# A graph-network kernel on one core: the three bf16 parts of the summed edge features are added once, and each graph-layer tile takes one edge product instead of two

## The reference, cut to what matters

```python
def _L2_gnn_ref(node_features, edge_index, edge_features, Ws, bs, gammas, betas):
    src, tgt = (edge_index[0], edge_index[1])
    x = node_features
    for i in range(NUM_LAYERS):                      # 3 layers
        msg = jnp.concatenate([x[src], edge_features], axis=-1)   # 10000 x (512 + 64)
        msg = msg @ Ws[i] + bs[i]
        agg = jax.ops.segment_sum(msg, tgt, num_segments=n)
        x = x + agg
        x = jax.nn.relu(_layer_norm(x, gammas[i], betas[i]))
    return x
```

## Time and profile before

| What | Value |
|---|---|
| Device time, median of 3 runs | 2346.91 us (2346.05 to 2350.74) |
| The profiled execution's own time | 2350.67 us |
| Its span in the trace | 2348.8 us |
| Mean granted clock of TensorE | 0.949 of full speed |
| TensorE (PE) busy | 2180.5 us, 93% |
| VectorE (DVE) busy | 1042.6 us, 44% |
| ScalarE (ACT) busy | 730.8 us, 31% |
| GpSimd (POOL) busy | 558.1 us, 24% |

### The profile page before, as it was taken

One profiled execution on the slowest core, in us unless ns is written; L12 is line 12 of the kernel. 1 busy time (PEld: TensorE's weight loads), 2 busy tenths in 40 slices (PEclk: granted clock), 3 DMA queues, 4 the chain that ended last, 5 costly groups with the idle time before them and its releaser, 6 DMA issues.

```text
span 2348.8 us, 21972 instructions
## 1 busy us (share of the span) xinstructions
PE 2180.5 (93%) x8167; PEld 1257.5 (54%) x8167; DVE 1042.6 (44%) x2142; ACT 730.8 (31%) x1221; POOL 558.1 (24%) x469
## 2 busy tenths in 40 slices
PE   6899886788899999997899999999999999999998
PEld 3576663677444555443455555555555544444443
DVE  8896675787323332344445345345344410000002
ACT  1576554676421210002143233233243111111110
POOL 4677764333211100010202202202202110022202
PEclk9999997787899969998899999999999899999999
DMA  9522204431020110005101101101101477787732
GB/s 344 159 34 34 28 4 108 129 86 57 1 94 19 54 54 20 1 0 187 64 10 55 67 10 59 64 9 59 54 1 54 172 262 302 284 303 307 288 152 70
DMA packets 61668, 238.26 MB, mean 101 GB/s; under 512 B 23375, under 2 KB 28451, under 8 KB 39436
## 3 DMA queue, kind: packets, MB, share of 16 engines
q1 hardware_dynamic: 32058, 169.04, 20.1%
q0 software_dynamic: 26336, 62.19, 8.6%
q10 hardware_dynamic: 3168, 5.63, 0.7%
HBM read 204.84 MB, written 31.96 MB: 101 GB/s over the span
## 4 chain that ended last, share of the span: by engine, by line
PE 64%; DVE 11%; issue 10%; POOL 4%; PEld 4%; DMA 3%; ACT 3%; SPq 0%; ACTq 0%; PEldq 0%; DVEq 0%; POOLq 0%
PE PS L995 10%; PE PS L725 10%; PE PS L718 7%; PE PS L1387 7%; PE PS L1396 6%; PE PS L1425 6%; PE PS L1293 3%; POOL pair_scores L1969 2%; PE PS L1033 2%; PE PS L1273 2%; DMA pair_scores<-TS,SIDX 2%; PE PS L736 1%; PEld PS L718 1%; DVE AR L2394 1%; PE PS L869 1%
## 5 line engine op out<-in xcount | busy, mean ns | idle before, releaser
L1940 POOL TENSOR_TENSOR RSTD<-VE,HALF 125x1 f32<-125x1 f32 x100 | 81.8, 818 | 1033.7 <-DVE VE L2101 1033.7
L995 PE MATMUL PS<-XT,WR 128*128 128x500 f32 (+2 forms) x992 | 235.5, 395 | 8.4 <-ACT XT L1493 4.4
L869 PE MATMUL PS<-HR,HOT 125*125 125x512 f32 x800 | 214.2, 416 | 19.2 <-DVE HOT L2245 17.6
L725 PE MATMUL PS<-WR,XT 128*125 128x512 f32 (+1 forms) x464 | 206.5, 592 | 14.1 <-DVE AR L2684 7.3
L2899 DVE TENSOR_TENSOR AR<-AR,PS 128x512 f32<-128x512 f32 (+1 forms) x44 | 30.3, 688 | 404.9 <-PE PS L1396 404.9
L995 PEld LDWEIGHTS PS<-XT,WR 128*128 128x128 f32 x992 | 145.7, 194 | 89.1 <-issue 74.5
L869 PEld LDWEIGHTS PS<-HR,HOT 125*125 125x125 f32 x800 | 148.6, 194 | 62.1 <-DVE HOT L2245 20.3
L1958 POOL DMA_INDIRECT pair_sums<-CW,SIDX x80 | 137.4, 1718 | 56.4 <-DMA pair_sums<-CW,SIDX 24.0
L725 PEld LDWEIGHTS PS<-WR,XT 128*125 128x125 f32 x464 | 86.8, 194 | 102.4 <-issue 85.5
L718 PE MATMUL PS<-XT,WR 128*128 128x113 f32 (+3 forms) x432 | 125.5, 447 | 1.8 <-DVE CW L2209 1.3
L2123 DVE TENSOR_TENSOR AR<-PS,AR 125x512 f32<-125x512 f32 x55 | 38.0, 692 | 189.3 <-PE PS L725 106.5
(11 more groups left out here) (422 smaller groups left out, 3995.1 us busy)
## 6 DMA issues: line engine op xcount, KB each, us to landing
WR<-in_qkv SPq DMA_DIRECT2D x12, 1024.0 KB
WR<-in_omm SPq DMA_DIRECT2D x12, 1024.0 KB
pair_scores<-CNT SPq DMA_DIRECT2D x1, 12212.0 KB, 36.0
AR<-pair_scores SPq DMA_DIRECT2D x5, 2187.5 KB
AR<-in_x_a SPq DMA_DIRECT2D x10, 1024.0 KB, 9.5
AR<-in_x_b SPq DMA_DIRECT2D x10, 1024.0 KB, 4.9
AR<-in_x_c SPq DMA_DIRECT2D x10, 1024.0 KB, 7.3
WR<-in_x_a SPq DMA_DIRECT2D x8, 1024.0 KB, 8.8
```

The source lines that it names most:

```text
L725: last = mm(s.ap[0:P, 0:cols], lhs, rhs, start=(k == 0), stop=(k == len(pairs) - 1))
L869: last = mm(DIFF[m % 4], HOT[g % 2][0:P, k, tile(j)], HR[0:P, k, :, b, :], start=(k == 0 and b == 0), stop=(k == NT - 1 and b == 1))
L995: last = mm(by_tile(s)[:, t0:t1, :], w[:, k, 128 * m:128 * (m + 1)], XT[:, k, P * t0:P * t1].rearrange("p (c n) -> p c n", n=P), start=(k ...
L1940: g.tensor_tensor(RSTD[:, t:t + 1], VE[:, t:t + 1], HALF[:, :], ALU.pow)\
```

## The change

ScalarE copies only the middle part to `EA1`, which shrinks to 64 rows at partitions 0 to 63, and `EA2` as before. VectorE waits for `graph_taken` and then makes two additions of 64 by 625 elements in place: the middle part to the low part in `EA2`, then the high part, read from PSUM. Each signals the new semaphore `graph_joined`, and TensorE waits for both in place of `graph_taken`. In the layers the product of line 1187 is gone, and the one with `EA2` opens each tile's sum. Two of the three loads of the edge rows are gone. The five semaphores `sums_in` become three, used in turn. The three parts are now added in float32 on VectorE in the place of TensorE's accumulation. The rounding of the first weights stays one unbroken loop.

```diff
--- before.py
+++ after.py
@@ -225,7 +225,7 @@
         G = G_ROWS[0:P, :, :]
 
 
-        EA1 = passing("EA1", [128, N])
+        EA1 = passing("EA1", [DH0, N])
         CONDR = sb("CONDR", [128, N], F32R)
         EA2 = sb("EA2", [128, N])
         with nc.sbuf_tensor("MODW_high", [128, D], F32):
@@ -431,9 +431,9 @@
         onehot_ready, onehot_used = sem("onehot_ready"), sem("onehot_used")
         graph_filled, graph_taken = sem("graph_filled"), sem("graph_taken")
         high_ready, middle_ready, low_ready = sem("high_ready"), sem("middle_ready"), sem("low_ready")
-        last_ready = sem("last_ready")
+        last_ready, graph_joined = sem("last_ready"), sem("graph_joined")
         edge_read = sem("edge_read")
-        sums_in = [sem(f"pair_sums_in_{t}") for t in range(NT)]
+        sums_in = [sem(f"pair_sums_in_{b}") for b in range(3)]
         sums_merged = sem("sums_merged")
         pairs_in = [sem("pair_scores_in_0"), sem("pair_scores_in_1")]
         scaled_ready, raw_filled, raw_taken = sem("scaled_ready"), sem("raw_filled"), sem("raw_taken")
@@ -565,7 +565,7 @@
                     for lo, hi in zip(WIDE_ROWS, WIDE_ROWS[1:]):
                         sp.dma_start(SUMS_IN[t][b][lo:hi].rearrange("p q c -> p (q c)"),
                                      pair_sums[b][N * (P * t + lo):N * (P * t + hi), :].rearrange(
-                                         "(p q) c -> p (q c)", q=N)).then_inc(sums_in[t], 16)
+                                         "(p q) c -> p (q c)", q=N)).then_inc(sums_in[t % 3], 16)
 
             def scores_of(t):
                 for lo, hi in zip(WIDE_ROWS, WIDE_ROWS[1:]):
@@ -601,8 +601,7 @@
                   (WR[:, 0, 2, 0:D], a["W2"])])
             load([mat(1, j, x) for j, x in enumerate(("e_W1", "e_W3", "e_W2"))])
             load([mat(0, j, "Wtop", j) for j in range(3)])
-            load([(WR[0:64, 1, 0, 0:3 * D], a["Wbot"]), (WR[64:128, 1, 0, 0:3 * D], a["Wbot"]),
-                  (WR[0:65, 1, 1, 0:3 * D], a["Wlast"])])
+            load([(WR[0:65, 1, 1, 0:3 * D], a["Wlast"])])
             load([mat(0, 0, "f_W1"), mat(0, 1, "f_W2"), (WR[0:8, 0, 2, 0:D], a["f_b2"])])
             def mod_rows(i, j, landed_in):
                 for r in range(4):
@@ -902,7 +901,7 @@
                                                    HR[0:P, t, h, :, :].rearrange("p b d -> p (b d)").bitcast(F32), ID[0:P, 0:P])
                     last.then_inc(s.filled, 1)
             all_taken("T")
-            pe.wait_ge(graph_taken, 1)
+            pe.wait_ge(graph_joined, 2)
 
 
             def quantized(u):
@@ -1181,11 +1180,10 @@
                     gathered.append((s, n.now(s.filled)))
                 if l == 0:
                     weights(0, 3)
-                    weights(1, 3)
+                    weights(1, 1)
                 for t in range(NT):
                     o = fill("N")
-                    mm(o.ap[0:P, :], EA1[:, tile(t)], WR[:, 1, 0, D * l:D * (l + 1)], start=True, stop=False)
-                    mm(o.ap[0:P, :], EA2[0:65, tile(t)], WR[0:65, 1, 1, D * l:D * (l + 1)], start=False, stop=False)
+                    mm(o.ap[0:P, :], EA2[0:65, tile(t)], WR[0:65, 1, 1, D * l:D * (l + 1)], start=True, stop=False)
                     for f in range(K4):
                         if t == 0:
                             copied(gathered[f])
@@ -1598,7 +1596,7 @@
                     fn(rows[:, :, tile(t)], s.ap[:, 0:4 * P].rearrange("p (h n) -> p h n", h=4), ACT.Copy)\
                         .then_inc(s.taken, 1)
             act.wait_ge(graph_filled, 1)
-            fn(EA1[:, :], PS[:, 2 * BANK:2 * BANK + N], ACT.Copy)
+            fn(EA1[0:DH0, :], PS[DH0:2 * DH0, 2 * BANK:2 * BANK + N], ACT.Copy)
             fn(EA2[0:65, :], PS[0:65, 4 * BANK:4 * BANK + N], ACT.Copy).then_inc(graph_taken, 1)
 
 
@@ -2303,7 +2301,7 @@
             for b in range(PARTS):
                 v.memset(S2[b][:, :, 64:65], 1.0)
             def merge(t):
-                dve.wait_ge(sums_in[t], 64)
+                dve.wait_ge(sums_in[t % 3], 64 * (t // 3 + 1))
                 one, two = SUMS_IN[t]
                 v.tensor_tensor(CNT[:, t, :], one[:, :, 0], two[:, :, 0], ALU.add)
                 v.tensor_tensor(G[:, t, :], one[:, :, 1], two[:, :, 1], ALU.add).then_inc(sums_merged, 1)
@@ -2344,6 +2342,10 @@
                     PRODUCT[rows, :].unsqueeze(2).unsqueeze(3).broadcast_to([DH0, HEADS0, 2, DH0]),
                     ALU.mult).then_inc(uv_ready, 1)
             psum.skip(T=2 * NT)
+            dve.wait_ge(graph_taken, 1)
+            for k, part_ in enumerate((EA1[0:DH0, :], PS[0:DH0, 2 * BANK:2 * BANK + N])):
+                v.tensor_tensor(EA2[0:DH0, :], EA2[0:DH0, :], part_, ALU.add).then_inc(graph_joined, 1)
+                dve.wait_ge(graph_joined, k + 1)
 
             def left(u):
```

## The result

| | before | after |
|---|---|---|
| median of four runs each (us) | 2346.77 | 2334.0 |
| lowest to highest (us) | 2346.05 to 2350.74 | 2332.2 to 2335.7 |
| profiled execution: its time, its span (us) | 2350.67, 2348.8 | 2333.17, 2331.4 |
| busy TensorE / VectorE / GpSimd (us) | | 2167.1 / 1043.0 / 553.4 |
| three graph layers, first edge product to the issue of `in_f_W` (us) | 120.86 | 107.98 |

What follows compares the result with a forecast made beforehand. TensorE was taken to bound the graph layers; -13.0 us for the products and +0.5 us for the additions gave -12.5 us, from a median of 2346.91 to 2334.4 us. The range was 2329 to 2341 us.

Steps and rivals of the forecast that it cites:

- The products: Graph layers, TensorE: 15 products go, each priced 0.87 us from start to start, -13.0 us.
- 65 rows at the price of 128: Graph layers: the product that stays has 65 rows for 128 and takes the same 592 ns, so nothing more is won.
- The copy and VectorE in the first two layers: First two layers: ScalarE's copy stays hidden by 2.5 us, VectorE's wait shrinks from 1.42 to 0.55 us; cost 0.
- The third layer: Third layer: VectorE becomes slower, `Y` comes 2.6 us later against TensorE, 5.7 us of slack remain; cost 0.
- if the wait for the weights shrinks by more than a us: Behind the layers: sign that the forecast is wrong, `Y` or something else having taken over.
- The loads and the semaphores: Two edge-row loads gone, TensorE waiting nowhere for their batch; three semaphores for five reads change no wait; cost 0.
- The additions at the hand-over: Behind the edge loop: 1.7 us of additions covered; GpSimd's stores stretched, +0.5 us, bounds -0.3 and +1.5.
- The cover: Hand-over: first kept group ready before GpSimd takes it at 382.61; 4.6 us of 6.4 left after the additions.
- Contention: Rival at the hand-over: additions and moved rounding block GpSimd's stores in full, +1.5 for +0.5, 2335.4 us; chance 8%.
- VectorE in the third layer: Rival: the tiles of `Y` are waited for behind the layers, 2.6 us given back, 2337.0 us; chance 7%.
- The clock of the heads: Rival, attention heads, 400 to 600 us: grant falls from 0.77 to below 0.71 and eats the gain; chance 3%.
- The product hidden: Rival in the layers: the removed product lay beside something ending at the same time, TensorE waits instead, 2346.9 us; chance 5%.

Runs made afterwards that it cites:

- e3: Kernel before without the 128-row `EA1` product in all three layers, no additions, all loads kept: layers 107.99 us, median 2328.95 us, ratio to before 0.9943.
- e9: Changed kernel with its 65-row `EA2` product issued twice per tile: layers 120.86 us, median 2341.32 us, ratio to before 0.9991.
- e1: Changed kernel with a 64-row `EA1` product put back per tile ahead of the `EA2` one: layers 126.51 us, median 2354.04 us, ratio to before 1.0052.
- e2: Kernel before with the `EA1` product left out in the third layer only, no additions: layers 116.56 us, median 2339.93 us, ratio to before 0.999.
- e8: Kernel before with the two additions, TensorE's wait and the three semaphores, both products and all loads kept: layers 120.86 us, median 2342.64 us, ratio 1.0005.
- e7: Changed kernel with the 65-row edge product in fp32r, sums and weights rounded: layers 98.67 us, median 2323.05 us, ratio to before 0.9916.
- e7b: Changed kernel with the edge product in fp32r, run a second time: layers 98.67 us, median 2320.84 us, ratio to before 0.9905.
- e0: Changed kernel unedited, run again for comparison within its group: layers 107.99 us, median 2326.09 us, ratio to before 0.9938.
- e6: Kernel before with the `EA1` product left out in the first two layers only, no additions: layers 112.27 us, median 2335.51 us, ratio to before 0.9974.
- e4: Changed kernel with six additions in place of two, TensorE waiting for the last: layers 107.98 us, median 2329.58 us, ratio to before 0.9925.
- e5: Changed kernel with 14 additions in place of two, TensorE waiting for the last: layers 107.98 us, median 2338.89 us, ratio to before 0.9988.
- e0b: Changed kernel unedited, a third time, for comparison within its group: layers 107.99 us, median 2328.71 us, ratio to before 0.9937.

## Why the prediction was right, and where it was off

The forecast was 2334.4 us, the measured median 2334.0. That they lie 0.4 us apart is in part luck: the interval of the ratio goes from -17.4 to -6.6 us, and the profiled execution, forecast at 2338.2, took 2333.17. What bears the forecast out is the length of the layers, -12.88 us for -13.0.

- **The products, -13.0 us:** the layers show -12.88, and `e3` -12.87 with nothing else changed; `e9` takes them back with one product of 0.87 us. That the records' sum (17.8 us) is too much and start to start counts is confirmed: 15 x 0.86.
- **65 rows at the price of 128:** holds, by `e9`. With 64 rows ahead of 65 it fails (`e1`).
- **The copy and VectorE in the first two layers, 0:** TensorE is never idle there, and VectorE's wait is 0.56 us, forecast 0.55.
- **The third layer, 0:** VectorE is the slower engine, as forecast. The third tile of `Y` was ready at 1053.51 + 0.54 = 1054.05 and turned at 1059.43, so 5.4 us of slack remained, forecast 5.7. `e2` shows the third layer's part, 4.30 us, arriving alone. The test I named for the opposite was badly put: "if the wait for the weights shrinks by more than a us" came true (6.53 to 4.05) and the theory stood. A wait can shrink because a shorter one has moved in ahead of it; the test should have been the distance from the issue to the first product, 9.22 and then 8.77 us.
- **The loads and the semaphores, 0:** the layers' first tiles are without idle time and `e8` with the semaphores is level with before. The loads were not tested alone.
- **The additions at the hand-over, +0.5 us:** each took 0.80 us, as priced by the earlier trace rows, and TensorE started 1.7 us later against the copy. But the term for GpSimd's stores was not there. In eight profiles with the two additions (the changed kernel's three, `e1`, `e7`, `e7b`, `e8`, `e9`) the stores that ran beside them took 0.95 to 0.96 us, as long as alone: all had begun before the first addition, or beside the second, which reads PSUM. The stretch to 1.25 us of the earlier trace rows, from which I took the size, is a matter of timing. It comes when a store begins within a step with two SBUF inputs: 1.44 us in `e0`, 1.08 to 1.09 in `e6`, `e7` and `e8`, none in after. Half a us is a tenth of what the medians can tell.
- **The cover, 4.6 us of 6.4:** this was mis-sized; it did not show in the sum because 1.7 us fit into either. In after 2.5 us are left (379.12 - 376.64), and 1.1 to 3.8 us in the eight profiles with two additions, where `e2`, `e3` and `e6` without them have 5.6 to 5.7.
- **What made the cover smaller:** I moved the whole rounding by 1.7 us and took its length from the one trace of before, where it was the shortest of all: from TensorE's start to the first kept group 376.25 - 369.59 = 6.66 us, at a granted clock of 1.00. It is 8.14 us at 0.81 in after, but also 7.85 to 8.28 us at 0.59 to 0.80 in `e2`, `e3` and `e6`, and 7.99 to 9.16 us with two additions. So the 3.9 us of cover that after lacks against before are 1.7 for the additions, 1.5 for the length of the rounding and 0.7 for the stores, which ended 12.5 us behind the copies and not 13.2. Behind the end of the copies the kept group came after 6.9 to 8.5 us without the additions (median 8.3, four profiles) and after 9.9 to 11.0 with two (median 10.0, eight profiles): 1.8 us later, forecast 1.7. `e4` and `e5` agree that the cover is smaller: GpSimd is late by 1.72 and 7.94 us, where 4.6 us of cover would have left none and 11.1 - 4.6 = 6.5. That TensorE's longer idle time, 3.92 us for 1.98, made the rounding slow is not shown. Its first eight products took 2.04 us in after and 1.13 in before, but behind 1.98 us of idle time they took 2.04 in `e3` too (and in `e6`), and behind 3.92 only 1.48 in `e7b`:

```profile
368.72 2.04 PE L929 MATMUL PS<-HRT_LOW,WR 128*128 128x125 f32 x8 [1.98 <-issue]
```

- **Rivals.** Contention: `e4` and `e5` show that it exists, with stores of 1.12 to 1.51 us beside an unbroken row of additions, each held to the end of the addition that was running when it began; beside two additions no store began within the first, and it was absent. The Trainium skill (SBUF — State Buffer, section "Who interferes with whom") has both: a VectorE instruction with two SBUF inputs contends with a GpSimd one that reads SBUF, and, as inferred, descriptor generation does not suffer from such an addition. These rows agree with the first, with 0.49 us of waiting for the 0.61 that were left; the second does not hold for these stores as a whole. They read their indices `SIDX`, and the rows don't tell that read from the descriptors' generation. VectorE in the third layer: it took over as the slower engine, but did not end the path. The clock of the heads: 162.53 us at 0.76, no fall. The product hidden: excluded by `e3`.

## What to carry to other kernels

Where an engine is busy without a gap through a stage, price a removed instruction from start to start and take it off; then check each engine beside it for the slack that is left, and the distance from the last issue to the next use rather than the length of one wait. Read a cover from several traces and not from one: here the stretch that the work was moved into took 6.66 us in the one trace of before and 7.85 to 8.28 in three others of its kind, and the forecast took the shortest. The height of a thin matmul is not free to choose: 65 and 128 rows cost the same here, and 64 ahead of 65 cost more.

## What the runs showed of the hardware

- A 64-row fp32 product of 512 columns between others took 1.05 us and made the next one 0.96, in place of 0.87 and 0.86; the load of weights waited 0.76 us for 0.24. Why was not tested.
- The same product of 65 rows in fp32r lengthens a tile by 0.24 us for 0.86 in fp32. The start of the fp32 product behind it is shown 0.64 us later and the following eight take 3.03 us for 3.43, so single records mislead here and the tile's length counts. What makes it shorter than the expected 0.43 was left open.
- The same eight small products of TensorE at the hand-over took 1.13 us in two profiles and 1.48 to 2.04 in the others. The length of the idle time before them does not order them: 1.98 us had 1.13 and 2.04 behind it, 3.92 us had 1.48 to 2.04. The granted clock from there to the first kept group was 1.00 in before and 0.50 to 0.82 in the others.
- A GpSimd store (an indirect DMA issue of 0.96 us) that begins while a VectorE step with two SBUF inputs runs waits for the rest of that step, less 0.12 us (1.45 us with 0.61 left, 1.12 with 0.28); beside a step with one input in PSUM it takes 0.96.
- The disturbance between VectorE and GpSimd goes both ways, and it isn't always the one that began first that goes on: in `e0b` a VectorE step of 0.69 us begun 0.21 us ahead of GpSimd's two-input product took 2.04. In `e5` a VectorE step of 0.69 us, begun 0.18 us into GpSimd's two-input product (390.41 to 391.67), took 1.63 and ended 0.55 us behind the product:

```profile
390.59 1.63 DVE L2366 SCALAR_TENSOR_TENSOR WR<-WR,BR 128x512 f32<-128x512 f32 x1 [0.26 <-ACT BR L1623]
```
